# Two-layer graph kernel on one core: both ends of an edge in one product, scalars and gates in one operation with a wider output tile, index columns copied by ScalarE, destinations as int16

## The reference

```python
xs = concat([x[src, :8], x[dst, :8]])                 # 16 scalars, 8 from each end
xv = concat([x[src, 8:], x[dst, 8:]])                 # 16 vectors of 3, 8 from each end
y1, y2 = _sph(edge_vec)                               # from the direction of the edge
h = sqrt(2) * relu(emb @ W1 / sqrt(10))               # 16 hidden values per edge
w = (h @ W2 / 4).reshape(E, 7, 16, 8)                 # 7 matrices of 16 x 8 per edge
s_out, g_out, v_out = ...                             # einsums of xs, xv, y1, y2 with w
s_act, gates = 1.593 * tanh(s_out), 1.593 * tanh(g_out)
edge_ftr = concat([s_act, gates[:, :, None] * v_out]) * norm
x = layernorm(x + segment_sum(edge_ftr, dst))
```

## Time and profile before

| | |
|---|---|
| median of 3 runs | 4478.09 us |
| the profiled execution, its time | 4480.86 us |
| its span | 4479.1 us |
| granted TensorE clock, mean | 0.956 |
| TensorE busy | 3332.8 us, 74% |
| VectorE busy | 3036.9 us, 68% |
| ScalarE busy | 2154.7 us, 48% |
| GpSimd busy | 3247.6 us, 73% |

### The profile page before, as it was taken

How to read it: one execution, slowest core, us unless ns; L and a number is a source line. 1 busy time by engine, 2 the same in 40 slices (tenths; PEclk the granted TensorE clock), 3 DMA queues, 4 the chain that set the end, 5 groups by cost and what they waited for, 6 DMA issues and landing times. The chain is left out here.

```text
span 4479.1 us, 67002 instructions
## 1 busy us (share of the span) xinstructions
PE 3332.8 (74%) x20487; PEld 2103.2 (47%) x20487; DVE 3036.9 (68%) x5225; ACT 2154.7 (48%) x4565; POOL 3247.6 (73%) x3440
## 2 busy tenths in 40 slices
PE   0003888888888888888888802999999999999940
PEld 0001332332332333233323202899999999999940
DVE  4433999999999999999999833344444444444432
ACT  3002555555555555555555310466666666666620
POOL 5776777777777777777777467777777777777766
PEclk9999999999999999999999955999999999999975
DMA  9612222222222222222222112133333333333311
GB/s 334 164 45 45 40 47 49 52 46 47 46 46 47 50 53 47 46 47 46 47 49 52 22 29 56 39 68 77 73 82 74 75 72 73 72 73 72 73 30 26
DMA packets 271192, 283.33 MB, mean 63 GB/s; under 512 B 182593, under 2 KB 236073, under 8 KB 268403
## 3 DMA queue, kind: packets, MB, share of 16 engines
q1 hardware_dynamic: 164150, 207.75, 16.8%
q0 software_dynamic: 106528, 70.98, 10.3%
q10 hardware_dynamic: 462, 4.00, 0.3%
HBM read 192.06 MB, written 90.42 MB: 63 GB/s over the span
## 5 line engine op out<-in xcount | busy, mean ns | idle before, releaser
L628 POOL DMA_INDIRECT edge<-xp_d,idx x1440 | 1420.8, 987 | 537.5 <-issue 393.6
L880 DVE TENSOR_TENSOR prod<-G_ps,hid 128x1000 f32<-128x1000 f32 x1200 | 1399.9, 1194 | 125.6 <-PE G_ps L763 111.3
L1275 POOL DMA_INDIRECT x1e<-tab_d,idxb x1122 | 1100.0, 980 | 342.2 <-issue 337.9
L763 PE MATMUL G_ps<-FT,wst 32*128 32x500 f32 x4800 | 896.6, 633 | 371.0 <-DVE prod L880 367.8
L1324 PE MATMUL G_ps<-tb,hot 128*126 128x442 f32 (+1 forms) x3968 | 799.1, 358 | 0.3 <-DVE x1e L1349 0.2
L1324 PEld LDWEIGHTS G_ps<-tb,hot 128*126 128x126 f32 x3968 | 743.0, 187 | 37.8 <-DVE x1e L1349 1.4
L763 PEld LDWEIGHTS G_ps<-FT,wst 32*128 32x128 f32 x4800 | 246.3, 183 | 807.4 <-DVE prod L880 750.7
L792 PE MATMUL R_ps<-prod,red 128*32 128x500 f32 x4800 | 590.5, 595 | 0.0
L684 ACT ACTIVATE hid<-T_ps 128x500 f32<-128x500 f32 x400 | 233.5, 584 | 721.5 <-PE T_ps L783 688.9
L1324 PE MATMUL T_ps<-tb,hot 128*126 128x442 f32 x2000 | 416.2, 360 | 186.3 <-DVE one_d L1408 186.3
L1324 PEld LDWEIGHTS T_ps<-tb,hot 128*126 128x126 f32 x2000 | 376.6, 188 | 204.9 <-issue 186.4
(11 more groups left out here) (235 smaller groups left out, 4369.5 us busy)
## 6 DMA issues: line engine op xcount, KB each, us to landing
xd_d<-zeros SPq DMA_DIRECT2D x16, 1562.5 KB, 28.6
y_d<-ng SPq DMA_DIRECT2D x40, 595.0 KB
edge<-xp_d,idx POOLq DMA_INDIRECT x1440
xv<-xd_d SPq DMA_DIRECT2D x40, 560.0 KB
y_d<-zr SPq DMA_DIRECT2D x40, 560.0 KB
x1e<-tab_d,idxb POOLq DMA_INDIRECT x1122
edge<-sel_d SPq DMA_DIRECT2D x20, 750.0 KB
edge<-sel_d SPq DMA_DIRECT2D x20, 687.5 KB
```

The lines of the kernel that those rows point to most:

```text
L628: nc.gpsimd.indirect_dma_start(out=edge_c[:, i, 8:8 + DIM], out_offset=None, in_=xp_d, in_offset=bass.IndirectOffsetOnAxis(col, 0)).then_i ...
L763: return Tn.matmul(G_ps[pair][:, a * 512:a * 512 + GW], wst[rows, r * 128:(r + 1) * 128], FT[k][rows, :], start=True, stop=True)
L880: V.tensor_tensor(prod[b][i][:, :].rearrange("p (a e) -> p a e", a=2), gv, hid[k][:, :].rearrange("p (a e) -> p a e", a=1).broadcast_to([1 ...
L1275: nc.gpsimd.indirect_dma_start(out=gx[b][:, c * T1:(c + 1) * T1], out_offset=None, in_=tab_d, in_offset=bass.IndirectOffsetOnAxis(idx[b][: ...
```

## The change

It has four parts, three in the edge loop and one in the first stage.

- *Both ends of an edge.* ScalarE writes the directions twice (`dr2`, once per chunk), and `turned` is one operation of 384 columns.
- *Post-processing.* `O` is widened from 32 to 40 features, the gates being features 8 to 15, and `pg` is gone. Scalars and gates are one operation of 128 columns. It and line 906 (now 907) write `O` with the column innermost, 8 consecutive values, and read `th` (64 bytes apart) and `pb` (96 bytes apart) in that order. `carry_sums` takes two copies.
- *Index columns.* `idx` is filled by ScalarE in `high`, and GpSimd neither copies nor waits for the copy.
- *First stage.* The destinations are also cast to int16, and the blocks that are fetched are of int16, 800 bytes per row.

```diff
-        dstf_d = dram("dstf_d", (NSB, SB))
+        dst16_d = dram("dst16_d", (NSB, SB), mybir.dt.int16)
...
-                        nc.gpsimd.indirect_dma_start(out=blkbuf[:, (k % NF) * SB:(k % NF + 1) * SB], out_offset=None, in_=dstf_d,
+                        nc.gpsimd.indirect_dma_start(out=blk16[:, (k % NF) * SB:(k % NF + 1) * SB], out_offset=None, in_=dst16_d,
...
                     V.tensor_copy(dstf[:, 1:], dst_i[:, :]).then_inc(S("a_dstf"), 1)
+                    V.tensor_copy(dst16[:, :], dst_i[:, :]).then_inc(S("a_dstf"), 1)
...
-                        V.tensor_scalar(junk[:, (k % NF) * SB:(k % NF + 1) * SB], blkbuf[0:P, (k % NF) * SB:(k % NF + 1) * SB], nodef[:, k:k + 1], None,
+                        V.tensor_scalar(junk[:, (k % NF) * SB:(k % NF + 1) * SB], blk16[0:P, (k % NF) * SB:(k % NF + 1) * SB], nodef[:, k:k + 1], None,
...
-                    act.wait_ge(S("a_dstf"), 1)
+                    act.wait_ge(S("a_dstf"), 2)
...
+            dr2 = two("dr2", C * 6)
...
-            O = two("O", C1 * DIM)
+            OW = DIM + MO
+            O = two("O", C1 * OW)
...
-                                if c == 0 and not fixed:
-                                    nc.gpsimd.tensor_copy(idx[:, i:i + PW], src_i[:, bass.ds((p + RING) * PW, PW)]).then_inc(S("b_ix"), 1)
-                                    hold(S("b_ix"), p - RING + 1)
...
+                        A.activation(dr2[h][:, :].rearrange("p (c d a) -> p c d a", d=2, a=3),
+                                     dr[h][:, :].rearrange("p (c d a) -> p c d a", d=1, a=3).broadcast_to([P, C, 2, 3]), ACT.Copy).then_inc(S("b_dr"), 1)
...
-                    def high(p, s, ch):
+                    def high(p, s, ch, fetch=False):
                         act.wait_ge(S("b_al"), p + 1)
+                        if fetch:
+                            A.activation(idx[:, s * PW:(s + 1) * PW], src_i[:, bass.ds((p + RING) * PW, PW)], ACT.Copy)
...
-                        nv = dr[h][:, c0 * 3:(c0 + PW) * 3].rearrange("p (c a u) -> p c a u", a=3, u=1).broadcast_to([P, PW, 3, 8])
-                        for d in range(2):
-                            ev = slot(s)[:, :, d * SD + 16:d * SD + 40].rearrange("p c (a u) -> p c a u", a=3)
-                            last = V.tensor_tensor(tmp[:, :].rearrange("p (c d a u) -> p c d a u", d=2, a=3, u=8)[:, :, d], ev, nv, ALU.mult)
-                        last.then_inc(S("b_tv"), 1)
+                        nv = dr2[h][:, c0 * 6:(c0 + PW) * 6].rearrange("p (e a u) -> p e a u", a=3, u=1).broadcast_to([P, 2 * PW, 3, 8])
+                        ev = edge[0:P, s * PW * EW:(s + 1) * PW * EW].rearrange("p (e f) -> p e f", f=SD)[:, :, 16:40].rearrange("p e (a u) -> p e a u", a=3)
+                        V.tensor_tensor(tv, ev, nv, ALU.mult).then_inc(S("b_tv"), 1)
...
-                            V.scalar_tensor_tensor(pgv, thv[:, :, 8:16], TG, nrm, ALU.mult, ALU.mult).then_inc(S("b_gs"), 1)
-                            V.scalar_tensor_tensor(ov[:, :, 0:8], thv[:, :, 0:8], TG, nrm, ALU.mult, ALU.mult).then_inc(S("b_gs"), 1)
+                            V.scalar_tensor_tensor(of[:, 0:2 * MO, :], thv[:, :, 0:2 * MO].rearrange("p c w -> p w c"), TG,
+                                                   nmp[h][:, c0:c0 + PW].rearrange("p (w c) -> p w c", w=1).broadcast_to([P, 2 * MO, PW]),
+                                                   ALU.mult, ALU.mult).then_inc(S("b_gs"), 1)
...
-                            V.tensor_tensor(ov[:, :, 8:32].rearrange("p c (w a) -> p c w a", a=3), pbv,
-                                            pgv.rearrange("p c (w a) -> p c w a", a=1).broadcast_to([P, PW, MO, 3]), ALU.mult).then_inc(S("b_o"), 1)
+                            V.tensor_tensor(of[:, 2 * MO:, :].rearrange("p (w a) c -> p w a c", a=3), pbv.rearrange("p c w a -> p w a c"),
+                                            of[:, MO:2 * MO, :].rearrange("p (w a) c -> p w a c", a=1).broadcast_to([P, MO, 3, PW]), ALU.mult).then_inc(S("b_o"), 1)
...
-                        V.tensor_copy(cols(O[h])[:, 0, :], cols(Z[1 - h])[:, C, :]).then_inc(S("b_cs"), 1)
+                        V.tensor_copy(cols(O[h])[:, 0, 0:MO], cols(Z[1 - h])[:, C, 0:MO])
+                        V.tensor_copy(cols(O[h])[:, 0, 2 * MO:], cols(Z[1 - h])[:, C, MO:]).then_inc(S("b_cs"), 1)
```

More of the change, by code:

```diff
@@ L149, in gnn_resnorm_kernel @@
         Y_ps = ctx.enter_context(nc.psum_tensor("Y_ps", [128, 512], f32))
-        src_i = sb("src_i", [PG, EP], i32)
+        src_i = sb("src_i", [PG, EP + 2 * PW], i32)
         idx = sb("idx", [PG, RING * PW], i32)
@@ L171, in gnn_resnorm_kernel @@
             dstf = sbt("dstf", [P, EP + 1])
+            dst16 = sbt("dst16", [P, EP], mybir.dt.int16)
             prev_i = sbt("prev_i", [P, 1], i32)
@@ L189, in gnn_resnorm_kernel @@
             fine = sbt("fine", [P, NP])
-            blkbuf = sbt("blkbuf", [PG, NF * SB])
+            blkbuf = sbt("blkbuf", [PG, 8 * P])
+            blk16 = sbt("blk16", [PG, NF * SB], mybir.dt.int16)
             w2s = sbt("w2s", [HID, 7 * 128])
@@ L452, in _ @@
                     by_rows(act, xn[:, :], x.rearrange("(p k) f -> p (k f)", k=NP), S("a_x"))
-                    act.wait_ge(S("a_dstf"), 1)
+                    act.wait_ge(S("a_dstf"), 2)
                     act.sem_inc(S("go"), 1)
-                    by_rows(act, dstf_d.rearrange("a b -> (a b)").rearrange("(p c) -> p c", c=EP), dstf[:, 1:], S("a_dstd"))
+                    by_rows(act, dst16_d.rearrange("a b -> (a b)").rearrange("(p c) -> p c", c=EP), dst16[:, :], S("a_dstd"))
                     act.wait_ge(S("a_xp"), 2)
@@ L527, in gnn_resnorm_kernel @@
             pb = sbt("pb", [P, PW * 24])
-            pg = sbt("pg", [P, PW * MO])
             NPC = DIM // 8
@@ L702, in turn @@
                                 s = (g + 4) // 2
-                                high(t * RING + s, s % RING, t * 2 + s // PC)
+                                high(t * RING + s, s % RING, t * 2 + s // PC, not last and not (first and s < RING))
                             if not (last and h == 1):
@@ L857, in turned @@
                             dve.wait_ge(S("b_dc"), ch * NPC + NPC)
-                            dve.wait_ge(S(f"b_ld{h}"), t * 128 + 128)
+                            dve.wait_ge(S("b_dr"), ch + 1)
                         if some(p):
@@ L896, in post @@
                                             ALU.mult).then_inc(S("b_pa"), 1)
-                            if some(m):
-                                dve.wait_ge(S("b_o"), m)
-                            V.scalar_tensor_tensor(pgv, thv[:, :, 8:16], TG, nrm, ALU.mult, ALU.mult).then_inc(S("b_gs"), 1)
-                            V.scalar_tensor_tensor(ov[:, :, 0:8], thv[:, :, 0:8], TG, nrm, ALU.mult, ALU.mult).then_inc(S("b_gs"), 1)
+                            V.scalar_tensor_tensor(of[:, 0:2 * MO, :], thv[:, :, 0:2 * MO].rearrange("p c w -> p w c"), TG,
+                                                   nmp[h][:, c0:c0 + PW].rearrange("p (w c) -> p w c", w=1).broadcast_to([P, 2 * MO, PW]),
+                                                   ALU.mult, ALU.mult).then_inc(S("b_gs"), 1)
                         if i == 1:
@@ L920, in sums @@
                         part = slice(i * 8 * C1, (i + 1) * 8 * C1)
-                        V.tensor_tensor_scan(out=Z[h][:, part], data0=kpp[h][:, :], data1=O[h][:, part],
+                        of = i if i == 0 else i + 1
+                        V.tensor_tensor_scan(out=Z[h][:, part], data0=kpp[h][:, :], data1=O[h][:, of * 8 * C1:(of + 1) * 8 * C1],
                                              initial=0.0, op0=ALU.mult, op1=ALU.add).then_inc(S(f"b_z{h}"), 1)
```

9 lines of the change are left out of this document (4 added, 5 removed).

## The result

| | |
|---|---|
| the changed kernel | 4496.74 us median (4492.33 to 4501.40, 6 runs) |
| the kernel before, on the same chip | 4477.85 us median (4474.99 to 4480.89, 6 runs) |
| ratio | 1.0041, 95% interval 1.0028 to 1.0054 |

The change makes the kernel slower by 0.4%. The forecast was 4472 us in a range of 4438 to 4485; the result lies outside the range and has the other sign.

What follows compares the result with a forecast made beforehand. In the edge loop TensorE was taken to end the even halves and VectorE to bound the odd ones. Terms -10 + 13 + 0 - 2 - 6 = -5 from 4480.86 gave 4476, 4473 on the median's scale; forecast 4472 us, range 4438 to 4485.

Steps and rivals of the forecast that it cites:

- cap for line 906: Odd half: the next product needs round2, so a shorter line 906 gains at most 0.14 us per piece.
- Part 1: Odd half, line 865: one operation of 384 columns instead of two of 192, 0.065 us less 160 times, -10 us.
- Part 2: Odd half, line 906: contiguous write but pb read at 96 bytes, 0.415 us, 0.065 more 200 times, +13 us.
- upper bound: Odd half, line 906: strided read at 0.9 ns more per column, making the term +18 us.
- rival A: Line 906: the 96-byte read is free, -17 in place of +13, 4443 us; chance 0.34.
- Rival C: Line 906 pays for both write and read, 0.50 us, +30 in place of +13, 4490 us; chance 0.08 with D.
- B: First stage gives back all its 22 us, the gated product as forecast: 4457 us; chance 0.08.
- D: Edge loop: ScalarE's new load or fuller DMA queues delay round starts, longer waits for th, 4 us; chance 0.08 with Rival C.
- Part 3: Even half: scalars and gates in one operation, carry_sums in two; the wait for TensorE takes it up, 0 us.
- Part 5: First stage: int16 destinations shorten gathers in the crowd, -7, second cast +1, net -6 us.
- Part 4: Edge loop: ScalarE copies index columns instead of GpSimd, which then stays ahead with its gathers; -2 us.

Runs made afterwards that it cites:

- turned kernel: Changed kernel with pa and pb stored edge innermost, so line 907 reads pb side by side: 4444.48 us, ratio 0.9925 to the kernel before.
- int16 alone: Kernel before with only the first stage's destinations as int16: 4479.47 us, ratio 0.9990.
- row of products: Changed kernel with 105 more VectorE operations of 192 columns, 21 forms of five, between edge loop and second layer, other engines pausing: 4536.19 us.

## Why the prediction was wrong

**What bounds the kernel** was read rightly. TensorE ended the even halves in every kernel here, with waits of 0.18 to 0.29 us in mid-loop (0.95 to 1.04 in the half without a scan), and what was done to VectorE in them changed nothing; the odd halves followed VectorE's operations one for one. Its cap for line 906 was worked out wrongly (1549.72 + 0.58 is 1550.30 and not 1550.36, so 0.20 and not 0.14 us), which nothing hung on: even the turned kernel's 0.27 us stays inside either.

**Part 1**, both ends in one product: 0.465 us was forecast, 0.46 measured. Two pairs of kernels differ by it and parts that don't touch the chunk: 54.09 (int16 alone, 1533.88 - 1479.79) and 53.72 us where GpSimd copies the index columns, 53.99 and 53.70 where ScalarE does. That is 0.29 to 0.37 us a chunk, 12 to 15 us in 40, against the forecast 10. (Over chunks 2 to 38 the second pair has means of 54.01 and 53.72, 0.29 as well.)

**Part 2** is the step that failed: the term of line 906, now 907. The 0.35 us for the old form was right (0.34 in the row of products, line 1025). For the strided read it took 0.15 us, "96 bytes is nearer to 132 than to 32". For 132 bytes the price was right: a product at that distance holds VectorE 0.40 us, 0.415 was taken. At 96 bytes it holds 0.53. The error is (0.53 - 0.415) x 200 = 23 us, and 4472 + 23 = 4495 is the result to within 2 us. That it fits so closely is partly luck: parts 1, 4 and 5 together gave some 8 us more than forecast (in the changed kernel's trace 2, 4 and 2), and the 4.8 us of scatter behind the loop took more than half of it back. The argument interpolated between two distances, 32 and 132 bytes, on a curve that rises above both in between. The 0.9 ns per column that stood as the upper bound was no bound either, since the rows of the trace held no read at 96 bytes; the true price is (0.53 - 0.27) / 192, 1.4 ns. Line 870, on which rival A rested, is a reduction with one input; a product with two pays at 32 bytes as at 128 (0.41 and 0.39 us), so the reduction's free read says nothing of the product's.

The row shows that reading at 8 bytes is free and at 16 is not. The Trainium skill states this rule ("Advanced Engine Details and Errata", "SBUF Cachelines"): lines of 16 bytes, and at least two hits on a line are needed to hide its latency. The runs of products agree at 8, 16 and 32 bytes. As that section states it, the rule makes no difference between 96 and 128 bytes, and there the measurement decides.

**Rival C** named the size (0.50 us, 4490) but not the mechanism: it had the written runs of 32 bytes cost 0.085 us on top of an ordinary strided read. They cost nothing; the read is dear. That the time came out near rival C's is luck of size. A and B did not come. D did not come either: ScalarE's `hid` still stood idle 0.24 us before its start in the tightest slot (1548.96), where it had 0.66.

**Part 3** was right at 0: line 898 takes 365 ns and the wait behind it is still 0.28 us. **Part 5** forecast -6, the trace has 7.9 and 8.5 us, the runs of it alone 4, with an interval of 0.4 to 8.5.

**Part 4** was forecast at -2. Alone it is 7 us by the ratio (2.7 to 10.7), 6.2 in the loop's trace: 2.7 for the wait, 1.2 at the loop's end and 2.4 since VectorE's instructions run slower beside GpSimd's copies, which the prediction didn't look for. With part 1 it is 26 us, as its sentence said in words only: without it parts 1 and 2 "would only turn into waits for gathers".

## What to carry to other kernels

Turning a layout inside an operation does not remove the stride, it moves it to the other operand, and the price must be known at the very distance that comes about: here eight neighbours at 96 bytes cost 0.26 us on top of a product of 0.27, at 128 bytes 0.12, and writing at 96 bytes 0.18. A tile of 24 words per entry is worth padding to 32, or better, worth writing in the order in which the operation on the critical path reads it, by an operation that has a wait behind it. And when one engine sets the pace by a hair, look at how far ahead its supplier is: relief of the supplier was worth 7 us alone and 26 us once the consumer was faster.

## What the runs showed of the hardware

- A VectorE product of 192 f32 columns, 125 rows, held its engine for 0.27 us with all operands side by side or with one input at 8 bytes, for 0.38 to 0.43 us with one input at any of 18 other distances from 16 to 480 bytes, and for 0.53, 0.46 and 0.44 us at 96, 100 and 104 bytes. Two inputs at 96 bytes cost no more than one. Nothing between 64 and 96 bytes was tried, and the cause is open.
- An operation with one input (`tensor_scalar`, 192 f32 columns) held VectorE for 0.24 us at 16 and 32 bytes and for 0.30 at 96.
- Written at a distance instead of read, the same product held 0.34 us at 164 bytes and 0.45 at 96, at both less than the read (0.41 and 0.53).
- A product that read PSUM at 256 bytes and SBUF side by side took 344 ns, as long as the one that read PSUM at 32 bytes (line 903, turned and changed kernel).
- A copy on VectorE of 32 columns took 225 and 204 ns on average in two kernels in which GpSimd copied 8 columns per piece, and 187 and 190 ns in the same two when it didn't (210 in a third that copied).
